# DLRM tower: GpSimd waits for the landing of one gather group before it issues the next

## The chip, the cores and the metric

The kernel runs on one core of one Trainium2 chip. The metric is device microseconds (us) of a whole execution. PE is TensorE, DVE is VectorE, ACT is ScalarE, POOL is GpSimd, SP is SyncE.

## The reference, cut to what matters

A batch of 2048 samples. Each has 26 ids, one into each embedding table (128 floats a row), and a dense vector of 128 floats. All in fp32:

```python
e = jnp.stack([tbl_f[ids[:, f]] for f in range(26)], axis=1)       # gather: 2048 x 26 x 128
combined = concatenate([dense[:, None, :], e], axis=1)             # 2048 x 27 x 128
z = einsum('bfd,bgd->bfg', combined, combined)[:, iu, ju]          # 351 pairs of each sample
h = relu(concatenate([z, dense], axis=1) @ W_top1 + b_top1)        # 479 -> 512
h = relu(h @ W_top2 + b_top2)                                      # 512 -> 256
y = h @ W_top3                                                     # 256 -> 1
```

## The kernel before

The batch is cut into 16 tiles of 128 samples. Two tiles (t = 0 and 1) make a turn s, and there are 8 turns. Turn 0 is written out; turns 1 to 7 run in a hardware loop on PE and ACT.

**Two kinds of features.** Ten tables of 1000 rows are "hot": they stay in SBUF, and PE fetches their rows by multiplying with one-hot matrices, for both tiles of the turn at once (`hot`, L449 to L463; 32 matmuls for each of 5 pairs of features, line L458). DVE makes the one-hot matrices (`compare`, L269 to L282, line L277). The other 16 tables are "cold": POOL gathers their rows from HBM by indirect DMA, one DMA of 128 rows for each tile and feature, into the one buffer `rows` (line L252, the loop L246 to L255). PE transposes these rows in `transposes` (L465 to L473, line L472), ACT copies what comes out to `feats` (L361 to L369).

**Groups.** `rows` holds 17 features of one tile: the dense vector (f = 0, loaded by SP, L193) and 16 cold ones. `GROUPS` (L40) cuts them in five: g0 has 3 gathers and the dense vector, g1, g2 and g3 have 4 gathers each, g4 has one. So a tile has 16 gathers and 5 groups, the whole kernel 256 gathers and 80 groups. Both tiles of a turn use the same `rows`: POOL may gather into group g of a tile when PE has transposed group g of the tile before (`wait_rows_free`, L154). Each group and tile of the turn has its own semaphore `gathered[t][g]`; each gather adds 16 to it when it has landed, and PE waits for it at L469.

**Order of the work.** It is written out by hand in `STEPS` (L56). In each turn PE does for tile 0: hot pair 0, rows g0, hot pair 1, rows g1 and so on to rows g4; then the first half of layer 1 (lines L496 to L498) of the turn before and the gram of tile 0. The gram is 512 small matmuls (L483). Then, for tile 1: rows g0, second half of layer 1 (of the turn before), rows g1, rows g2, layer 2 (L540), rows g3, rows g4, layer 3 (L548), and the gram of tile 1. ACT works through the same list with its copies, with the relu (L378) behind each layer. Behind each gram ACT and DVE copy the products out, and SP moves the pairs to `pairs` by nine DMAs (L176); SP also loads the ids of the next turn (L189). PE transposes groups g3 and g4 of tile 1 only after layer 2.

**What POOL does.** Only the gathers and the waits in front of them. All waits are conditions on semaphores that others raise; no other engine waits for POOL but by the landing of its gathers.

**The names below.** "Chain of gathers of turn s": POOL's gathers for tile 0 of turn s. It begins when PE has transposed group g0 of tile 1 of turn s - 1. The chains begin at 55.68, 118.09, 179.59, 238.81, 297.44, 355.94 and 414.16 us for turns 1 to 7.

Of the kernel before, what the change touches and what calls it, by code (L numbers as in the profile page):

```python
# [8 lines left out]
def dlrm_tower(nc, ids, dense, tables, ident, hot_ids, hot_tables, hot_rows, w1, b1, w2, b2, w3, out):  # L9
# [30 lines left out]
    GROUPS = [list(range(g, min(g + 4, NR))) for g in range(0, NR, 4)]  # L40
    NG = len(GROUPS)
# [19 lines left out]
    with ctx:  # L61
# [3 lines left out]
        def sem(name):  # L65
            return ctx.enter_context(nc.semaphore(name))
# [42 lines left out]
        gathered = [[sem(f"gathered{t}_{g}") for g in range(NG)] for t in range(2)]  # L109
# [40 lines left out]
        def wait_rows(eng, s, t, g):  # L150

            eng.wait_ge(rows_done, 2 * NG * s + NG * t + g + 1)

        def wait_rows_free(eng, s, t, g):  # L154

            if t == 1:
                wait_rows(eng, s, 0, g)
            elif s > 0:
                wait_rows(eng, s - 1, 1, g)
# [14 lines left out]
        def move_pairs(eng, t, pieces):  # L174
            for c, p0, n, j0, w in pieces:
                eng.dma_start(pairs[p0:p0 + n * w, c, t * P:(t + 1) * P],  # L176
                              gram[0:n, (j0 - 1) * P:(j0 - 1 + w) * P].rearrange(
                                  "i (j b) -> i j b", j=w)).then_inc(pairs_in[t], 16)
# [4 lines left out]
        @block.sync  # L183
        def _(sp):
            def load_ids(s, part):
                a, b = ((0, IDS_A), (IDS_A, NH))[part]
                if s > 0:
                    sp.wait_ge(compared, NH * (s - 1) + b)
                sp.dma_start(ids_b[:, a:b, :].rearrange("p f b -> p (f b)"),  # L189
                             hot_ids[s:s + 1, a * SB:b * SB].to_broadcast([P, (b - a) * SB])).then_inc(  # L190
                                 ids_in[part], 16)

            def load_dense(s, t):  # L193
                wait_rows_free(sp, s, t, 0)
                sp.dma_start(rows[:, 0, :], dense[2 * s + t, :, :]).then_inc(dense_in[t], 16)

            def wait_gram(s, t):
                if s == 0 and t == 0:
                    sp.wait_ge(zeroed, 1)
                elif s > 0:  # L200
                    sp.wait_ge(pairs_split, s)
                for h in range(2):
                    sp.wait_ge(gram_out[h], 4 * (2 * s + t + 1))

            def load_table(f):
                src = hot_tables[f].rearrange("(p c) d -> p c d", c=HC)
                for a, b in ((0, 112), (112, HP_ROWS)):
                    sp.dma_start(hot_raw[a:b, f, :, :], src[a:b, :, :]).then_inc(raw_in[f], 16)  # L208

            sp.dma_start(hot_rows_sb[0:HP_ROWS, :], hot_rows).then_inc(hot_rows_in, 16)  # L210
            sp.dma_start(idx[:, :, :], ids).then_inc(idx_in, 16)
            sp.dma_start(ident_sb[:, :], ident).then_inc(ident_in, 16)
            load_ids(0, 0)
            load_table(0)
            load_table(1)
            load_table(2)
            load_dense(0, 0)
            load_table(3)
            load_ids(0, 1)
            for f in range(4, NH):  # L220
                load_table(f)
            sp.dma_start(w1_raw, w1.rearrange("(c p) n -> p c n", p=P)).then_inc(raw_w1_in, 16)
            sp.dma_start(w2_sb[:, :, :], w2.rearrange("(c p) n -> p c n", p=P)).then_inc(weights_in, 16)
            sp.dma_start(w3_sb[:, :], w3).then_inc(weights_in, 16)
            sp.dma_start(b1_sb[:, :], b1).then_inc(weights_in, 16)
            sp.dma_start(b2_sb[:, :], b2).then_inc(weights_in, 16)

            for s in range(TURNS):
                load_dense(s, 1)
                if s + 1 < TURNS:  # L230
                    load_ids(s + 1, 0)
                wait_gram(s, 0)
                move_pairs(sp, 0, PIECES)
                if s + 1 < TURNS:
                    load_ids(s + 1, 1)
                    load_dense(s + 1, 0)
                wait_gram(s, 1)
                move_pairs(sp, 1, PIECES if s + 1 < TURNS else LAST_HERE)
            sp.wait_ge(y_out, TURNS)
            sp.dma_start(out, y).then_inc(stored, 16)  # L240
            sp.wait_ge(stored, 16)

        @block.gpsimd
        def _(pool):
            pool.wait_ge(idx_in, 16)
            for s in range(TURNS):  # L246
                for t in range(2):
                    for g, features in enumerate(GROUPS):
                        wait_rows_free(pool, s, t, g)
                        for f in features:  # L250
                            if f > 0:
                                pool.indirect_dma_start(  # L252
                                    out=rows[:, f, :], out_offset=None, in_=tables[f - 1],
                                    in_offset=bass.IndirectOffsetOnAxis(ap=idx[:, 2 * s + t, f - 1:f], axis=0),
                                ).then_inc(gathered[t][g], 16)  # L255
# [407 lines left out]
```

## Time and profile before

| | |
|---|---|
| median of 3 runs | 511.42 us (511.13 to 512.32) |
| the profiled execution, its own time | 512.17 us |
| its span, first to last instruction | 510.4 us |
| mean granted TensorE clock | 0.839 of full |
| PE busy | 360.0 us (71%), 6224 matmuls |
| DVE busy | 242.9 us (48%) |
| POOL busy | 254.2 us (50%), 256 of its 260 instructions gathers |
| ACT busy | 153.6 us (30%) |
| HBM read | 29.97 MB, 59 GB/s over the span |

Busy time is the time in which an engine has an instruction at work. A wait is put down to the instruction that released it; "remote" means that the profile found none that could have, "issue" that nothing it shows was waited for. The busy time of a gather on POOL is the making of its descriptors; the data move afterwards.

### The profile page before, as it was taken

Reading aid. Unit: us, or ns where it says so; the run is one execution under the profiler, and the core shown is the slowest. Engines: PE = TensorE matmul, PEld = TensorE weight load, DVE = VectorE, ACT = ScalarE, POOL = GpSimd, SP = SyncE. Lnnn points to the kernel's source line nnn. Section 1 sums busy time; section 2 is a strip of 40 time slices with the busy share of each in tenths; the row PEclk is TensorE's granted clock in tenths of the full one; section 3 lists DMA queues with packets and bytes.
Section 4 is the critical chain, followed back from the end, with each engine's and each line's share of the span. In section 5 each row is a group of like instructions: output and inputs, shape, how many; then the busy total and the mean of one; then the engine's idle time right before and its main releaser. Section 6 shows DMA issues by size and latency. Waiting matters only on the chain.

```text
span 510.4 us, 13987 instructions
## 1 busy us (share of the span) xinstructions
PE 360.0 (71%) x6224; PEld 332.2 (65%) x6224; DVE 242.9 (48%) x172; ACT 153.6 (30%) x269; POOL 254.2 (50%) x260
## 2 busy tenths in 40 slices
PE   7695516977279763989369782897459882798927
PEld 6583406966179762989259781896439881797826
DVE  4995703827048270745429370673509451380220
ACT  2462401234122331324132241233232341223512
POOL 5887560655506474265635755264734745165000
PEclk9988656999569995899759986898959986698978
DMA  7992230211202131121303112131312112111000
GB/s 198 251 278 54 55 90 7 79 43 51 78 17 80 36 87 46 34 65 39 94 26 77 46 45 79 29 74 31 102 31 66 47 41 84 26 54 41 16 15 1
DMA packets 23322, 33.32 MB, mean 65 GB/s; under 512 B 6565, under 2 KB 15397, under 8 KB 23303
## 3 DMA queue, kind: packets, MB, share of 16 engines
q0 software_dynamic: 8192, 16.79, 12.6%
q1 hardware_dynamic: 14926, 16.20, 11.8%
q8 instruction: 12, 0.20, 0.2%
q10 hardware_dynamic: 186, 0.09, 0.1%
q14 instruction: 6, 0.05, 0.0%
HBM read 29.97 MB, written 0.01 MB: 59 GB/s over the span
## 4 chain that ended last, share of the span: by engine, by line
PE 56%; issue 18%; another core or an unknown queue 14%; ACT 7%; DMA 3%; SPq 2%; DVE 1%; ACTq 0%; DVEq 0%
PE psum L458 31%; PE psum L483 11%; PE psum L472 3%; DMA lows<-table 3%; ACT feats L336 3%; PE psum L548 3%; PE psum L496 2%; PE psum L497 2%; PE psum L498 2%; ACT gram L336 2%; PE psum L540 1%; ACT h L378 1%; SPq L208 1%; ACT dense_hi L336 1%
## 5 line engine op out<-in xcount | busy, mean ns | idle before, releaser
L252 POOL DMA_INDIRECT rows<-table,idx x256 | 254.0, 992 | 215.0 <-PE psum L472 114.2
L277 DVE TENSOR_TENSOR onehot<-ids_b,psum 125x2048 fp32r<-125x2048 int16 x80 | 180.2, 2283 | 18.5 <-PE psum L458 12.3
L260 DVE COPY gram<-psum 26x416 f32<-26x416 f32 x64 | 37.4, 584 | 182.6 <-PE psum L483 181.1
L336 ACT ACTIVATE feats<-psum 128x512 f32<-128x512 f32 (+1 forms) x120 | 77.4, 689 | 148.1 <-PE psum L458 106.9
L458 PE MATMUL psum<-onehot,hot_hi 125*128 125x256 f32 x640 | 99.2, 299 | 11.1 <-issue 6.8
L483 PE MATMUL psum<-feats 128*26 128x26 f32 x4096 | 64.3, 211 | 59.6 <-issue 55.7
L483 PEld LDWEIGHTS psum<-feats 128*26 128x26 f32 x4096 | 55.9, 125 | 70.8 <-issue 64.8
L458 PE MATMUL psum<-onehot,hot_lo 125*128 125x256 f32 x640 | 95.6, 291 | 4.4 <-issue 4.3
L458 PEld LDWEIGHTS psum<-onehot,hot_hi 125*128 125x128 f32 x640 | 86.5, 200 | 14.2 <-issue 9.0
L458 PEld LDWEIGHTS psum<-onehot,hot_lo 125*128 125x128 f32 x640 | 86.7, 198 | 6.3 <-issue 5.6
L336 ACT ACTIVATE gram<-psum 26x416 f32<-26x416 f32 (+1 forms) x72 | 35.5, 494 | 73.1 <-PE psum L483 54.5
L548 PE MATMUL psum<-h,w_sb 128*1 128x256 f32 x32 | 13.2, 560 | 60.2 <-ACT h L378 60.2
L378 ACT ACTIVATE h<-psum,b_sb 128x256 f32<-128x256 f32 x44 | 18.4, 470 | 102.2 <-remote 78.4
L548 PEld LDWEIGHTS psum<-h,w_sb 128*1 128x1 f32 x32 | 2.5, 99 | 66.4 <-ACT h L378 62.2
L472 PE MATMUL psum<-ident_sb,rows 128*128 128x128 f32 x272 | 42.0, 282 | 0.0
L496 PE MATMUL psum<-pairs_hi,w_hi 126*128 126x256 f32 (+1 forms) x96 | 28.5, 297 | 9.0 <-DVE pairs_lo L286 9.0
L472 PEld LDWEIGHTS psum<-ident_sb,rows 128*128 128x128 f32 x272 | 32.9, 145 | 1.2
L540 PE MATMUL psum<-h,w_sb 128*128 128x256 f32 x128 | 29.0, 379 | 0.0
L286 DVE TENSOR_TENSOR pairs_lo<-pairs,pairs_hi 126x768 fp32r<-126x768 f32 x8 | 7.9, 987 | 43.3 <-ACT pairs_hi L336 34.3
L497 PE MATMUL psum<-pairs_lo,w_hi 126*128 126x256 f32 (+1 forms) x96 | 28.2, 294 | 0.0
L498 PE MATMUL psum<-pairs_hi,w_lo 126*128 126x256 f32 (+1 forms) x96 | 28.1, 293 | 0.0
L540 PEld LDWEIGHTS psum<-h,w_sb 128*128 128x128 f32 x128 | 23.7, 190 | 2.9
(26 smaller groups left out, 167.7 us busy)
## 6 DMA issues: line engine op xcount, KB each, us to landing
lows<-table SPq DMA_DIRECT2D x10, 448.0 KB
rows<-table,idx POOLq DMA_INDIRECT x256, 2.5
ids_b<-hot_ids SPq DMA_DIRECT2D x8, 384.0 KB
ids_b<-hot_ids SPq DMA_DIRECT2D x8, 256.0 KB
rows<-dense SPq DMA_DIRECT2D x16, 64.0 KB
lows<-w SPq DMA_DIRECT2D x1, 1024.0 KB
pairs<-gram SPq DMA_DIRECT2D x16, 39.0 KB
lows<-table SPq DMA_DIRECT2D x10, 52.0 KB
```

Source lines behind the costliest of these rows:

```text
L252: pool.indirect_dma_start(out=rows[:, f, :], out_offset=None, in_=tables[f - 1], in_offset=bass.IndirectOffsetOnAxis(ap=idx[:, 2 * s + t, ...
L260: return nc.vector.tensor_copy(o, x)
L277: nc.vector.tensor_tensor(onehot[f % SLOTS][0:HP_ROWS, :, :], ids_b[0:HP_ROWS, f:f + 1, :].to_broadcast([HP_ROWS, HC, SB]), psum[0:HP_ROWS ...
L336: return nc.scalar.activation(o, x, ACT.Copy)
L458: mm = nc.tensor.matmul(psum[:, bank, (f % 2) * SB:(f % 2 + 1) * SB], part[0:HP_ROWS, f, c, :], onehot[f % SLOTS][0:HP_ROWS, c, :], start= ...
L472: mm = nc.tensor.transpose(psum[:, bank, m * P:(m + 1) * P], rows[:, f, :], ident_sb[:, :])
L483: mm = nc.tensor.matmul(psum[32 * q:32 * q + NJ, GP[h], k * NJ:(k + 1) * NJ], feats[:, t, n, 0:NJ], feats[:, t, n, 1:NF], start=True, stop ...
L496: nc.tensor.matmul(o, w_hi, x_hi, start=(n == 0), stop=False)
L497: nc.tensor.matmul(o, w_hi, x_lo, start=False, stop=False)
L498: return nc.tensor.matmul(o, w_lo, x_hi, start=False, stop=(n == ZC))
L540: mm = nc.tensor.matmul(psum[:, HP[0], m * SB:(m + 1) * SB], w2_sb[:, c, m * P:(m + 1) * P], h1[:, c, :], start=(c == 0), stop=(c == C1 - 1))
L548: mm = nc.tensor.matmul(psum[0:1, HP[1], 0:SB], w3_sb[:, m:m + 1], h2[:, m, :], start=(m == 0), stop=(m == C2 - 1))
```

## The change

POOL gets one more wait at the head of each group. `wait_landed` waits until all gathers of the group in front of it (in POOL's order, across tiles and turns too) have added their 16 to their semaphore. The first group of all has none in front.

```diff
         @block.gpsimd
         def _(pool):
+            def wait_landed(s, t, g):
+
+                if g > 0:
+                    t0, g0, s0 = t, g - 1, s
+                else:
+                    t0, g0, s0 = 1 - t, NG - 1, s - (t == 0)
+                if s0 >= 0:
+                    pool.wait_ge(gathered[t0][g0], 16 * sum(f > 0 for f in GROUPS[g0]) * (s0 + 1))
+
             pool.wait_ge(idx_in, 16)
             for s in range(TURNS):
                 for t in range(2):
                     for g, features in enumerate(GROUPS):
                         wait_rows_free(pool, s, t, g)
+                        wait_landed(s, t, g)
                         for f in features:
                             if f > 0:
                                 pool.indirect_dma_start(
```

## Rows read from the trace of the kernel before

**Rows 1.** The page: shares of the chain that ended last.

```profile
PE 56%; issue 18%; another core or an unknown queue 14%; ACT 7%; DMA 3%; SPq 2%; DVE 1%; ACTq 0%; DVEq 0%
```

**Rows 2.** The page's costliest groups: busy us, mean ns of one | idle before, releaser.

```profile
L252 POOL DMA_INDIRECT rows<-table,idx x256 | 254.0, 992 | 215.0 <-PE psum L472 114.2
L483 PE MATMUL psum<-feats 128*26 128x26 f32 x4096 | 64.3, 211 | 59.6 <-issue 55.7
L378 ACT ACTIVATE h<-psum,b_sb 128x256 f32<-128x256 f32 x44 | 18.4, 470 | 102.2 <-remote 78.4
```

**Rows 3.** Waits: who waited for whom, us in total, times, longest.

```profile
POOL rows L252 <- PE psum L472: 114.2, 21, 14.4
POOL rows L252 <- remote: 30.1, 13, 3.0
```

**Rows 4.** Timeline of POOL in turn 4, to turn 5's next chain: start us, us, what [idle before].

```profile
297.44 0.94 POOL L252 DMA_INDIRECT rows<-table,idx  x1 [5.10 <-PE psum L472]
...
299.94 0.94 POOL L252 DMA_INDIRECT rows<-table,idx  x1 [0.30 <-issue]
301.19 0.94 POOL L252 DMA_INDIRECT rows<-table,idx  x1 [0.30 <-issue]
...
310.25 0.95 POOL L252 DMA_INDIRECT rows<-table,idx  x1 [0.30 <-issue]
314.18 0.94 POOL L252 DMA_INDIRECT rows<-table,idx  x1 [2.98 <-remote]
...
319.18 0.94 POOL L252 DMA_INDIRECT rows<-table,idx  x1 [0.30 <-issue]
328.73 0.94 POOL L252 DMA_INDIRECT rows<-table,idx  x1 [8.61 <-PE psum L472]
...
350.05 0.94 POOL L252 DMA_INDIRECT rows<-table,idx  x1 [0.30 <-issue]
355.94 0.94 POOL L252 DMA_INDIRECT rows<-table,idx  x1 [4.94 <-PE psum L472]
```

**Rows 5.** Line L252: gathers from issue (start on POOL) to landing.

```profile
DMA to landing us min/median/max: 2.5/2.5/4.4
```

**Rows 6.** Timeline of PE in the same stretch.

```profile
304.22 0.71 PE L472 MATMUL psum<-ident_sb,rows 128*128 128x128 f32 x5
314.77 1.44 PE L548 MATMUL psum<-h,w_sb 128*1 128x256 f32 x3 [9.84 <-ACT h L378]
...
316.43 0.71 PE L483 MATMUL psum<-feats 128*26 128x26 f32 x35
317.57 0.33 PE L483 MATMUL psum<-feats 128*26 128x26 f32 x6 [0.43 <-issue]
...
321.16 2.59 PE L483 MATMUL psum<-feats 128*26 128x26 f32 x200 [1.11 <-issue]
...
327.85 0.60 PE L472 MATMUL psum<-ident_sb,rows 128*128 128x128 f32 x4
```

**Rows 7.** Timeline of ACT in the same stretch: the relu behind layer 2.

```profile
313.88 0.84 ACT L378 ACTIVATE h<-psum,b_sb 128x256 f32<-128x256 f32 x2 [9.68 <-remote]
```

**Rows 8.** Timeline of PE in the last turn, with POOL at rest.

```profile
480.41 0.71 PE L472 MATMUL psum<-ident_sb,rows 128*128 128x128 f32 x5
481.50 1.02 PE L548 MATMUL psum<-h,w_sb 128*1 128x256 f32 x4 [0.38 <-ACT h L378]
482.43 2.56 PE L483 MATMUL psum<-feats 128*26 128x26 f32 x256
```

**Rows 9.** Timeline of POOL: chains of turn 1 and turn 7, first and last gathers.

```profile
6.21 0.95 POOL L252 DMA_INDIRECT rows<-table,idx  x1 [0.30 <-issue]
...
55.68 0.94 POOL L252 DMA_INDIRECT rows<-table,idx  x1 [3.69 <-PE psum L472]
...
74.41 0.94 POOL L252 DMA_INDIRECT rows<-table,idx  x1 [0.30 <-issue]
...
414.16 0.94 POOL L252 DMA_INDIRECT rows<-table,idx  x1 [4.86 <-PE psum L472]
...
468.43 0.94 POOL L252 DMA_INDIRECT rows<-table,idx  x1 [0.30 <-issue]
```

**Rows 10.** Timeline of PE in turn 0: first transposes, and the gram of tile 1.

```profile
15.71 0.60 PE L472 MATMUL psum<-ident_sb,rows 128*128 128x128 f32 x4
...
58.98 0.55 PE L483 MATMUL psum<-feats 128*26 128x26 f32 x42 [1.12 <-ACT feats L336]
...
78.71 2.34 PE L483 MATMUL psum<-feats 128*26 128x26 f32 x179 [0.50 <-issue]
```

**Rows 11.** Stretch 5 to 38 us: busy PE, PEld, DVE, ACT, POOL; clock, DMA share, GB/s.

```profile
5.00:38.00 33.00, 27.16 (x180) 24.98 (x178) 30.25 (x19) 15.62 (x18) 26.60 (x22) 0.95 1.04 264
```

## The prediction

> **What bounds the kernel now.** I read the chain of waits first. Only 56% of it is PE at work; 18% is "issue" and 14% an unknown queue [rows 1]. So the span holds a good part in which PE has nothing to do that the program names. The costliest groups say where: the gram matmuls sat 55.7 us in "issue", and ACT's relu waited 78.4 us for something "remote" [rows 2]. POOL is busy only half the span, and it waited 114.2 us for PE's transposes and 30.1 us for "remote" [rows 3]. Now the timelines of turn 4. PE's records put layer 2 and the transposes of g3 and g4 of tile 1 before 304.93 (304.22 + 0.71) [rows 6], but ACT's relu, which needs only layer 2, starts at 313.88 [rows 7], and POOL, which needs only the g3 transposes, at 314.18 [rows 4]. Two engines agree: what PE finished by 304.9 was not seen until about 313.9, 9 us later. Then the gram of tile 1, 256 matmuls, runs in scraps (35, 6, ... matmuls with gaps) and gets free only at 321.16 [rows 6].
>
> The last turn runs the same loop code on PE, but there POOL is at rest: its last gather is issued at 468.43 [rows 9]. There layer 3 follows the transposes of 480.41 at 481.50, with no hold, and the gram takes 2.56 us in one piece [rows 8]. DVE's comparisons and SP's id loads for a next turn are absent there too, so this contrast alone does not say which of them is to blame. The second sign is better: the scraps follow POOL. In turn 4 the hold ends 3.6 us after the last gather of an unbroken run (310.25 to 313.88), the gram is free 2.0 us after the next run's last one (319.18 to 321.16) [rows 4, 6, 7]. In turn 0 the gram of tile 1 starts freely at 58.98, is cut off at 59.53, and gets free at 78.71, 4.3 us after the last of 16 dense gathers (74.41) [rows 9, 10]: some 20 us for 2.6 us of work. And it begins late: the cut comes 3.85 us after that run's first gather (55.68 to 59.53), in turn 4 3.0 us after (314.18 to 317.14) [rows 4, 6, 9, 10]. So I read: an unbroken run of gathers stalls PE, from 3.0 to 3.85 us after its first issue until 2.0 to 4.3 us after its last. How, no row says.
>
> **The change, part by part.** Nothing is removed. POOL gets 79 waits. Inside a run, gathers start 1.25 us apart (299.94 to 301.19, over a group's edge) [rows 4]. With the wait, the next group's first starts after the landing of the last one before: 2.5 us by the median [rows 5], and a wake-up, for which I take POOL's 0.28 us behind PE's transposes (327.85 + 0.60 to 328.73) [rows 4, 6]. That is 2.75, so 1.5 us more for each group edge, 79 x 1.5 = 119 us in all. Bounds for one landing: 2.5 and 4.4 us [rows 5]. Behind POOL's wait only gathers are queued; who waits for them is PE's transposes alone.
>
> The Trainium skill (DMA: Bandwidth & Descriptors, Anatomy of one DMA, SWDGE path) gives a GpSimd DMA about 2.0 us fixed plus bytes over 436 GB/s, an estimate of 2.15 us for a gather of 64 KB. The trace has 2.5, a little more, and that is used; by the page's figure POOL's floor below would be 80 x 0.35 = 28 us lower.
>
> POOL's own floor: a tile has 16 gathers in 5 groups, 11 steps of 1.25 and 5 of 2.75 = 27.5 us; a turn has 55.0. Some gathers take longer than 0.944 us (the total of 254.0 is 12.3 us above 256 x 0.944 [rows 2, 4]), most in turn 0; I add 0.5 a turn: 55.5. Now a turn takes 355.94 - 297.44 = 58.5 us [rows 4]. So POOL, which had slack, becomes the bound, yet below today's turn, if PE keeps up. Would it? After the change a group's last issue is followed by 2.75 us of nothing and then at least 3.0 us before a cut: a free stretch from 2.0 to 4.3 until 5.75 to 6.6 us behind each last issue, 1.5 to 4.6 us of each 6.5. That releases the held layer 2 (due at 304.9) at the edge it falls on instead of after 9 us, and gives the gram its 2.6 us in one or two pieces. PE's turn without the hold (9.0) and with the gram of tile 1 at 2.6 instead of the 7.3 from 316.43 to 323.75 [rows 6] is 58.5 - 9.0 - 4.7 = 44.8 us, 11 under POOL's 55.5. I take it that PE keeps up.
>
> Start: POOL begins at 3.6 and has two tiles of 27.5: 58.6. Between 5 and 38 us the DMA engines are full (share 1.04, 264 GB/s) [rows 11], and landings are late: g0's last was issued at 6.21 and had landed by 15.71 at the latest [rows 9, 10], so 2.5 to 9.5 us. Four edges lie there. I take 5.0 each, nearer the middle since at most four gathers then stand in the queue: +10; stretched gathers +4. Chain of turn 1 at 72.6 (bounds 58.6 to 91) against 55.68: +17.
>
> Turns 1 to 6: 6 x 55.5 = 333.0 against 414.16 - 55.68 = 358.5 [rows 9]: -25.5. Turn 7's chain to its last landing: 55.2 against 468.43 + 2.5 - 414.16 = 56.8: -1.6. Then the tail. Before, PE transposes the last groups at 481.12, 10.2 us after the last landing, because it was late itself [rows 8, 9]; after, it is waiting for them and does so 0.9 us after the landing: -9.3. From there to the end the same 29.3 us. Sum: +17 - 25.5 - 1.6 - 9.3 = -19.4. Against the profiled execution's 512.17 (span 510.4 and 1.8 around it) 492.8; this execution stands 0.75 above the median of the runs, so **492 us**.
>
> **The rivals.**
> (a) Landings come later than the median. From this case's sum: 0.1 us on each landing costs 7 us over 7 turns of 10 edges, so from 2.5 + 19.4/70 = 2.8 us on the kernel is slower than before. The 4.4 of [rows 5] is for it, that the median equals the minimum is against it. At 3.0 us it gives 492 + 35 = 527.
> (b) The pauses don't free PE, since it takes a rest longer than they leave (the 4.3 us of turn 0 is for it, the 2.0 and 3.6 of turn 4 and the late cut against). Then each edge is added to the path: the end of the hold moves by two edges (3.0), the gram's release by three (4.5), and the gram of tile 0, which waits out the run that ends at 350.05, by 8.6 (those 4.5 and four edges more, 6.0, less 1.9 that lie in POOL's waits) [rows 4, 6]. A turn takes 67, and 512 + 6.5 x 8.6 + 10 for the start = 578. It decides from the point where a run's stall outlasts the 5.75 us.
> (c) Same: PE is held by something else (DVE's comparisons, the id loads), and 1.5 us at an edge fits in POOL's 144 us of waits [rows 3]; but not all of the edges lie beside them. 508 to 516.
> (d) Landings get shorter when fewer gathers are under way, or the start costs nothing: 475 to 480.
>
> The Trainium skill (same page, Rules for kernel authors) says to issue a DMA early and to wait for it late, so that the fixed cost overlaps. The change waits at once, 79 times. Rivals (a) and (b) are what that rule would give here. The trace agrees with it in that the extra POOL time is real, and disagrees in that the dense issue has a price of its own on PE.
>
> **How the numbers follow.** The forecast case 0.55, with a range of its own of 480 to 508 (landings 0.1 us either way, the start 10 us either way); (a) 0.18, (b) 0.13, (c) 0.09, (d) 0.05. Runs of this kernel can tell 0.2% (1 us) from no change. Faster: 0.55 + 0.05 and 0.02 of (c) = 0.62; the same 0.05; slower 0.18 + 0.13 + 0.02 of (c) = 0.33. The range runs from 480 to 538: it takes in most of (a) and all of (c), and leaves out (b) and (d).
>
> **What would show it.** In POOL's timeline: starts 2.7 to 2.8 us apart at every group edge, waits that end on a landing and hardly any on PE's transposes. A chain every 55.5 us. ACT's relu behind layer 2 within 3 us of PE's record of it, the 78.4 us of "remote" gone to under 30, the gram's 55.7 us of "issue" under 25. PE idle before the transposes instead, and a lower granted clock. In turn 0 the chain of turn 1 begins near 72.6. It is wrong if POOL still waits for PE at the g3 group (rival b), if edges measure 3 us or more (rival a), or if the relu is held as before with POOL pausing (rival c).

## The result, and the profile after

The changed kernel takes 549.41 us (median of 4 runs, 549.14 to 554.35), the kernel before 511.87 us beside it (4 runs, 511.13 to 512.34): a ratio of 1.0761, 95% interval 1.0708 to 1.0815. It is slower by 7.6%. The forecast was 492 us and faster; the time is also above the range.

The profiled execution of the changed kernel took 554.35 us, with a span of 552.5. The chain of waits, where [rows 1] had PE at 56%:

```profile
DMA 36%; POOL 26%; issue 19%; PE 17%; SPq 1%; DVE 1%; ACT 0%; POOLq 0%; DVEq 0%; ACTq 0%
```

The end is now set by POOL's gathers and their landings. The costliest groups (against [rows 2]; busy us, mean ns of one | idle before, releaser):

```profile
L262 POOL DMA_INDIRECT rows<-table,idx x256 | 247.8, 968 | 272.9 <-DMA rows<-table,idx 166.3
L493 PE MATMUL psum<-feats 128*26 128x26 f32 x4096 | 82.7, 211 | 79.8 <-issue 76.5
L388 ACT ACTIVATE h<-psum,b_sb 128x256 f32<-128x256 f32 x44 | 18.4, 470 | 44.2 <-PE psum L508 21.1
```

The waits, us in total, times, longest (against [rows 3]):

```profile
POOL rows L262 <- DMA rows<-table,idx: 166.3, 61, 7.3
...
PE psum L482 <- DMA rows<-table,idx: 57.2, 20, 5.9
...
POOL rows L262 <- PE psum L482: 34.2, 13, 4.7
```

POOL waits 166.3 us for landings and hardly for PE: of the 13 waits put down to PE, 11 are edges of 3.2 to 3.4 us like those put down to a landing (at 395.90 below, for one). PE waits 57.2 us for gathered rows, which it did not before. POOL's timeline in turn 4 (start us, us, what [idle before]), against [rows 4]:

```profile
333.70 0.94 POOL L262 DMA_INDIRECT rows<-table,idx  x1 [2.26 <-PE psum L482]
...
336.20 0.94 POOL L262 DMA_INDIRECT rows<-table,idx  x1 [0.30 <-issue]
339.43 0.94 POOL L262 DMA_INDIRECT rows<-table,idx  x1 [2.29 <-DMA rows<-table,idx]
...
350.19 0.96 POOL L262 DMA_INDIRECT rows<-table,idx  x1 [0.30 <-issue]
354.37 0.94 POOL L262 DMA_INDIRECT rows<-table,idx  x1 [3.23 <-DMA rows<-table,idx]
...
395.90 0.94 POOL L262 DMA_INDIRECT rows<-table,idx  x1 [2.35 <-PE psum L482]
```

Over a group's edge the starts are 3.23 us apart (336.20 to 339.43), at the worst edge of the tile 4.18 (350.19 to 354.37). The turn takes 395.90 - 333.70 = 62.2 us (the mean of turns 1 to 6 is 63.3), where it took 58.5 before and 55.5 in the forecast. PE at the same time (against [rows 6]):

```profile
333.98 0.73 PE L493 MATMUL psum<-feats 128*26 128x26 f32 x43
335.02 0.24 PE L493 MATMUL psum<-feats 128*26 128x26 f32 x3 [0.32 <-issue]
335.74 0.26 PE L493 MATMUL psum<-feats 128*26 128x26 f32 x5 [0.48 <-issue]
...
337.91 1.86 PE L493 MATMUL psum<-feats 128*26 128x26 f32 x142 [1.16 <-issue]
340.00 0.30 PE L493 MATMUL psum<-feats 128*26 128x26 f32 x5 [0.23 <-issue]
```

The gram of tile 1 is still in scraps, some five matmuls in each 0.73 us while a group's gathers are issued. In POOL's pause after 336.20 it runs freely from 337.91 to 339.77, and is cut 0.6 us after the next group's first gather (339.43 to 340.00). Its first 43 ran freely beside gathers too. (A gram is 256 matmuls, 4096 for 16 tiles; the 512 given in the description of the kernel are those of a turn.)

The start of the run, the chain of turn 7 and the last gather (against [rows 9]):

```profile
6.20 0.94 POOL L262 DMA_INDIRECT rows<-table,idx  x1 [0.30 <-issue]
14.40 0.94 POOL L262 DMA_INDIRECT rows<-table,idx  x1 [7.25 <-DMA rows<-table,idx]
...
79.35 0.94 POOL L262 DMA_INDIRECT rows<-table,idx  x1 [2.26 <-PE psum L482]
...
459.20 0.94 POOL L262 DMA_INDIRECT rows<-table,idx  x1 [2.26 <-PE psum L482]
...
520.15 0.94 POOL L262 DMA_INDIRECT rows<-table,idx  x1 [4.66 <-PE psum L482]
```

The prediction's terms against the two profiled executions:

| term | forecast | measured |
|---|---|---|
| chain of turn 1 begins later | +17 | 79.35 - 55.68 = +23.7 |
| turns 1 to 6 | -25.5 | 379.85 - 358.48 = +21.4 |
| chain of turn 7 to its last landing (last issue + 2.5) | -1.6 | 63.45 - 56.8 = +6.7 |
| tail | -9.3 | 29.9 - 39.5 = -9.6 |
| sum | -19.4 | +42.2 (spans: 552.5 - 510.4 = 42.1) |

The profiled execution stands 4.9 us above the median, so the medians are 37.5 apart.

**Two times of the kernel before.** One thing must be known to read the experiments. In most of the later comparisons the kernel before took 382 to 387 us, not 512. In the first measurement, in that of `each` (513.89) and in that of `small_compare`, `nogather_b`, `latechain_b` and `two_ahead_b` (510.83) it took 508 to 515. Within a comparison it never changed (9 and 13 runs in two of them), so ratios hold inside one. The number of the chip doesn't tell the two apart (number 6 gave 384.10 once and 510.83 later). I call them the 512 place and the 385 place. Of the 127 us between them PE's busy time makes 23 (360.0 us in the 512 place, at a granted clock of 0.839; 336.8 in `extra` below, the stand-in for the kernel before in the 385 place, at 0.964); the rest is time in which PE sits idle. The gathers land in 2.5 us by the median in both. What makes the two places is open.

### The profile page after: what moved, and what is told of

Read it like the earlier page. It is cut to its first block, busy times and chain, and to the rows that moved or that the text cites. A ratio compares the mean times of both kernels' runs of the same rounds, so it can differ in the third digit from the quotient of the medians.

```text
span 552.5 us, 14062 instructions
## 1 busy us (share of the span) xinstructions
PE 393.6 (71%) x6224; PEld 355.3 (64%) x6224; DVE 242.9 (44%) x172; ACT 154.8 (28%) x269; POOL 248.0 (45%) x260
## 4 chain that ended last, share of the span: by engine, by line
DMA 36%; POOL 26%; issue 19%; PE 17%; SPq 1%; DVE 1%; ACT 0%; POOLq 0%; DVEq 0%; ACTq 0%
DMA rows<-table,idx 35%; POOL rows L262 26%; PE psum L468 9%; PE psum L493 3%; PE psum L482 2%; PE psum L558 1%; PE psum L550 1%; SPq L176 1%; DMA pairs<-gram 1%; PE psum L506 0%; DVE gram L270 0%; DMA idx<-ids 0%; PE psum L507 0%; PE psum L508 0%; DVE pairs_lo L296 0%
## 5 line engine op out<-in xcount | busy, mean ns | idle before, releaser
L262 POOL DMA_INDIRECT rows<-table,idx x256 | 247.8, 968 | 272.9 <-DMA rows<-table,idx 166.3
L493 PE MATMUL psum<-feats 128*26 128x26 f32 x4096 | 82.7, 211 | 79.8 <-issue 76.5
L493 PEld LDWEIGHTS psum<-feats 128*26 128x26 f32 x4096 | 64.3, 124 | 99.4 <-issue 93.8
L468 PE MATMUL psum<-onehot,hot_hi 125*128 125x256 f32 x640 | 104.7, 311 | 5.4 <-DVE onehot L287 2.5
L468 PEld LDWEIGHTS psum<-onehot,hot_hi 125*128 125x128 f32 x640 | 92.4, 213 | 8.3 <-DVE onehot L287 4.5
L482 PE MATMUL psum<-ident_sb,rows 128*128 128x128 f32 x272 | 50.8, 312 | 57.9 <-DMA rows<-table,idx 57.2
L482 PEld LDWEIGHTS psum<-ident_sb,rows 128*128 128x128 f32 x272 | 35.6, 157 | 64.7 <-issue 30.2
L388 ACT ACTIVATE h<-psum,b_sb 128x256 f32<-128x256 f32 x44 | 18.4, 470 | 44.2 <-PE psum L508 21.1
L506 PEld LDWEIGHTS psum<-pairs_hi,w_hi 126*128 126x128 f32 (+1 forms) x96 | 21.8, 227 | 9.1 <-DVE pairs_lo L296 9.1
L550 PEld LDWEIGHTS psum<-h,w_sb 128*128 128x128 f32 x128 | 23.7, 190 | 2.9
L507 PEld LDWEIGHTS psum<-pairs_lo,w_hi 126*128 126x128 f32 (+1 forms) x96 | 21.7, 226 | 0.1
L508 PEld LDWEIGHTS psum<-pairs_hi,w_lo 126*128 126x128 f32 (+1 forms) x96 | 21.5, 224 | 0.0
```

Source lines behind the costliest of these rows:

```text
L262: pool.indirect_dma_start(out=rows[:, f, :], out_offset=None, in_=tables[f - 1], in_offset=bass.IndirectOffsetOnAxis(ap=idx[:, 2 * s + t, ...
L388: nc.scalar.activation(dst[:, c, :], psum[:, bank, n * SB:(n + 1) * SB], ACT.Relu, bias=bias[:, c:c + 1]).then_inc(relu_out, 1)
L468: mm = nc.tensor.matmul(psum[:, bank, (f % 2) * SB:(f % 2 + 1) * SB], part[0:HP_ROWS, f, c, :], onehot[f % SLOTS][0:HP_ROWS, c, :], start= ...
L482: mm = nc.tensor.transpose(psum[:, bank, m * P:(m + 1) * P], rows[:, f, :], ident_sb[:, :])
L493: mm = nc.tensor.matmul(psum[32 * q:32 * q + NJ, GP[h], k * NJ:(k + 1) * NJ], feats[:, t, n, 0:NJ], feats[:, t, n, 1:NF], start=True, stop ...
L506: nc.tensor.matmul(o, w_hi, x_hi, start=(n == 0), stop=False)
```

## Experiments

The theories after the result. Theory 1: the term for a group's edge was too small, since the new wait is an instruction of its own, where the one that it was priced from rides on a gather; POOL's turn sets the time. Theory A: a dense run of gathers stalls PE. Its rivals: DVE's comparisons, the id loads or memory traffic do. The expectations number their theories anew for each run; where that matters, the text says which is meant. Of the code of each edit only the lines that matter are shown.

**again.** The changed kernel, nothing edited, with others beside it.

> The changed kernel once more, beside the kernel before, since on the chip of the runs 'swap' to 'latechain' the kernel before took 385 us and not 512. Theory A (the change makes POOL the bound, on any chip): 545 to 555 us here too, with group edges of 3.2 us, whatever the kernel before takes. Theory B (the changed kernel is slow only where PE is stalled): it moves with the kernel before, to about 1.07 of it, 413 us where that takes 385.

549.18 us (547.08 to 554.2), before 384.10: ratio 1.4279 (1.4217 to 1.4341). The changed kernel takes 549 us in both places, and the kernel before doesn't. In the 385 place its grams hardly wait (6.2 us of "issue" for 76.5), and its time is the same: what PE gains there doesn't shorten POOL's chain. The chain of waits at one edge (start us, us, what):

```profile
383.46 2.53 DMA rows<-table,idx
385.99 0.02 issue
386.02 0.02 POOLq L252
386.03 0.72 issue
386.75 0.94 POOL rows L262
```

The landing is seen at 385.99; the wait (its line is L252) is an instruction of its own and ends at once; the next gather starts 0.76 us after the landing.

**swap and swap_b.** The same wait, one line higher.

```diff
-                        wait_rows_free(pool, s, t, g)
                         wait_landed(s, t, g)
+                        wait_rows_free(pool, s, t, g)
```

> The changed kernel with its two waits at the head of a group in the other order: landing first, transposes second. Nothing else differs. Theory 1: a group edge of 3.25 us (last issue to next group's first) is 2.5 us of landing and 0.74 us because the landing wait is an instruction of its own in front of the gather (record of it 0.74 us before the gather's start), while the wait on the transposes rides on the gather itself and costs only 0.28 us. In the other order the landing wait rides on the gather: edges of 2.8 us, 79 x 0.45 = 36 us less, about 514 us. Theory 2: a landing always costs POOL 0.75 us until the next start, in whatever form it is waited for: edges stay at 3.25, 549 us.

> The change with its two waits in the other order, once more. Theory A: POOL's turn sets the time of this kernel, so it takes 505 to 511 wherever it runs; where the kernel before takes 512 that is about the same or 1% faster. Rival: where PE is stalled beside dense gathers, this kernel loses to it as well, and takes 530 or more there. Where before takes 385 it gives 508 as in the first run of it, and tells nothing new.

508.02 us (506.08 to 509.87), before 385.39: ratio 1.3194 (1.3136 to 1.3252). The second time 506.64 (506.23 to 509.08), before 384.37: 1.3203 (1.3133 to 1.3273); it met the 385 place again, so its question stays open. Where two waits are written ahead of a gather, the first rides on the gather and the second becomes an instruction of its own: in the changed kernel the landing wait, here the wait for PE. The edge of `swap`:

```profile
250.78 0.94 POOL L262 DMA_INDIRECT rows<-table,idx  x1 [0.30 <-issue]
253.54 0.94 POOL L262 DMA_INDIRECT rows<-table,idx  x1 [1.81 <-DMA rows<-table,idx]
```

2.76 us, the landing of 2.5 and 0.26. Nothing else was edited, and the kernel is 41 us faster than `again`, both in the 385 place (36 were expected). Theory 1 holds. Both kernels have 75 waits that are instructions of their own; in `swap` they hardly ever block. The changed kernel has one such edge itself, in tile 0 of turn 0, where there is no wait for PE yet and the landing wait rides:

```profile
42.23 0.94 POOL L262 DMA_INDIRECT rows<-table,idx  x1 [0.30 <-issue]
44.96 0.94 POOL L262 DMA_INDIRECT rows<-table,idx  x1 [1.78 <-DMA rows<-table,idx]
```

2.73 us there, 3.2 and more at all edges behind it. Why a wait of its own takes half a microsecond more, the trace doesn't show.

**extra.** The kernel before with a wait at each group's head that is always met.

```diff
                         wait_rows_free(pool, s, t, g)
+                        pool.wait_ge(idx_in, 16)
```

> The kernel before, with one more wait at the head of each group, on the ids of the gathers, which landed at the start: the instruction without any waiting. Theory 1 (a separate wait instruction costs the gather behind it 0.4 to 0.5 us): the start-to-start distance over a group edge grows from 1.25 to about 1.7 us, and the time by 0 to 10 us, since POOL had waits of 144 us: 512 to 522 us. Theory 2 (the price belongs to the landing): edges stay at 1.25 to 1.3 us and the time at 511.9.

384.55 us, before 385.39: 0.9996 (0.9971 to 1.0022). Group edges stay 1.25 us. So the first expectation for this run, that the mere instruction widens an edge to 1.7 us, missed. A wait of its own costs nothing if it doesn't block; the 0.76 us fall due when it does. This run is also the trace for the kernel before in the 385 place:

```profile
PE 336.8 (88%) x6224; PEld 311.5 (82%) x6224; DVE 241.2 (63%) x172; ACT 152.7 (40%) x269; POOL 253.0 (66%) x260
...
PE 77%; POOL 9%; issue 7%; DMA 2%; ACT 2%; SPq 1%; DVE 1%; POOLq 0%; DVEq 0%; ACTq 0%
...
L484 PE MATMUL psum<-feats 128*26 128x26 f32 x4096 | 55.6, 195 | 12.9 <-issue 4.6 <-ACT feats L337 3.3
```

PE is busy 88% of the span and makes 77% of the chain.

**less_pe.** The changed kernel without half of the one-hot matmuls.

```diff
-                    for part in (hot_hi, hot_lo):
+                    for part in (hot_hi,):
```

> The changed kernel with half of the one-hot matmuls (those with hot_lo, 640 of 6224, 92 to 96 us of PE's busy time) left out in all turns. Theory A (POOL's chain of issues and landings sets the time): 540 to 550 us, within 2% of the changed kernel. Rival (PE is a bound too, its stalls or its clock): 10 us or more of the 92 come back for each 10% that PE holds, under 535 us.

552.62 us, before 384.73: 1.437 (1.4231 to 1.4509). PE's busy time falls from the 374.3 of `again` to 321.2 us and the kernel gains nothing. PE is no bound of the changed kernel in the 385 place. In the 512 place this edit wasn't run; there the chain of waits and the equal time of 549 us say the same.

**small_ids.** The changed kernel with the id loads of turns 1 to 7 cut to one partition.

```diff
-                sp.dma_start(ids_b[:, a:b, :].rearrange("p f b -> p (f b)"),
+                rows_to = P if s == 0 else 1
+                sp.dma_start(ids_b[0:rows_to, a:b, :].rearrange("p f b -> p (f b)"),
```

> The changed kernel, with the id loads of turns 1 to 7 (384 and 256 KB, spread over 128 partitions) cut to one partition; DVE compares stale ids there. Theory A: the landings of 3.0 to 4.1 us instead of 2.5, one or two in each tile, are late because of these loads: they go, 14 times 0.9 = 13 us less, 536 us. Rival: they are late beside the moves of the pairs (nine DMAs of SP, 7.2 us, by 512 bytes): unchanged, 549 us.

547.83 us, before 384.84: 1.4235 (1.3978 to 1.4492). The late landings (3.0 to some 4 us, one or two a tile) stay, so the id loads don't make them. They lie in SP's stretch of pair moves, as in the changed kernel in turn 4, from 348.24 on, with the edge of 354.37 in it:

```profile
348.24 7.26 SPq L176 DMA_DIRECT2D pairs<-gram  x9
```

That these moves delay the landings wasn't tried.

**two_edges.** The kernel before with the landing wait of the change at two edges a turn, from turn 1 on.

```diff
+                        if t == 0 and g in (1, 2) and s > 0:
+                            wait_landed(s, t, g)
```

> The kernel before with landing waits at only two edges of a turn: in front of g1 and g2 of tile 0, where the trace of 512 us showed PE held for 9 us. Each costs POOL 2.0 us. Where the kernel before takes 385 us, PE is not held and POOL's waits for PE are under 4 us a turn: 4 us a turn on POOL show up at most in part, 385 to 410. Where it takes 512: theory A, pauses free PE: the held relu comes up to 5 us earlier, 480 to 505; theory B, they don't: 3 to 4 us later per turn, 530 to 540.

402.38 us, before 384.06: 1.0482 (1.039 to 1.0575). 18.3 us for 14 edges, 1.3 each: even 14 of the 79 waits cost. The question for the 512 place, whether two pauses free PE, wasn't met.

**two_ahead and two_ahead_b.** The wait for the group two in front, ahead of `wait_rows_free`.

```diff
+                n = 2 * NG * s + NG * t + g - 2
+                s0, t0, g0 = n // (2 * NG), n // NG % 2, n % NG
```

> The changed kernel waiting for the group two in front (so two groups may be under way), landing wait first. A group of four takes 5.0 us to issue, longer than the 2.5 us of a landing; only behind g4, which has one gather, a wait of 1.25 us is left: POOL turns of 40 + 2.5 us, no bound. Theory A (the price is POOL's alone): within 1% of the kernel before on the same chip. Rival (any landing wait costs the path): 3% or more above it.

> The wait for the group two in front. Where before takes 512: if the stall comes from gathers being dense, not from how many are under way, 500 to 525, for the gathers stay 1.25 us apart. Rival (outstanding gathers stall PE): below 450. Where before takes 385: 394.

385 place: 394.33 us, before 384.10: 1.0265 (1.0236 to 1.0293). 512 place: 526.50, before 510.83: 1.032 (1.0234 to 1.0406). The first lies between the theories' 1% and 3%, the second just above the 500 to 525 of its first theory and far from the rival's 450. Most edges are back at 1.25 us; behind the lone gather of g4, where only one gather lies between the wait and what it waits for, they are 1.5 to 2.5 in the 385 place. In the 512 place the grams still sit 64.6 us in "issue". So limiting POOL to two groups frees nothing. It doesn't test how many single gathers may be under way: with 1.25 us from issue to issue and 2.5 us to a landing there are about two, here as in the kernel before.

**nogather and nogather_b.** The kernel before with the gathers of turn 0 only; PE waits for those alone.

```diff
-            for s in range(TURNS):
+            for s in range(1):
```

> The kernel before without the gathers of turns 1 to 7; PE's transposes wait only for those of turn 0, so turns 1 to 7 work on stale rows. All of DVE, ACT, SP and PE is the same. Theory 1 (gathers under way stall PE): no 9 us between PE's record of layer 2 and ACT's relu, grams of 2.6 us in one piece, turns of about 45 us instead of 58.5: some 420 us. Rival (the comparisons on DVE or the id loads hold PE): the 9 us and the scraps stay, turns of 55 us or more, above 485 us.

> The kernel before without the gathers of turns 1 to 7 (they use turn 0's rows). Theory A: about 370 us whatever before takes on this chip, grams in one piece. Rival (comparisons or id loads stall PE): about 500 where before takes 512. Where before takes 385, 370 as in the run of this kernel before, which tells nothing more.

385 place: 370.01 us, before 385.39: 0.9596 (0.9564 to 0.9628). 512 place: 371.68, before 510.83: 0.7285 (0.7206 to 0.7365). The 420 us first expected were reckoned for the 512 place before the other was known; the second expectation, 370, came true. Without gathers the two places are the same within 0.5%. The comparisons and the id loads are all there, and the grams don't stall. So the gathers, directly or by what hangs on them, make all of the difference between 385 and 512.

**small_compare.** The kernel before with the comparisons of turns 1 to 7 cut to an eighth.

```diff
+                n = HC if first else 1
-                    onehot[f % SLOTS][0:HP_ROWS, :, :],
+                    onehot[f % SLOTS][0:HP_ROWS, 0:n, :],
```

> The kernel before with DVE's comparisons of turns 1 to 7 cut to an eighth of their columns (so the one-hot matrices are not made anew there). The question is what holds PE's small matmuls where the kernel before takes 512 us. Theory A: dense gathers do; then this stays near 500 or more where before takes 512, with PE's grams still in scraps. Rival: the comparisons do, then the time falls toward 390 and the grams run in one piece. Where before takes 385, PE is the bound and this gives 380 to 385, which tells nothing of the question.

509.51 us, before 510.83, both in the 512 place: 0.996 (0.9922 to 0.9998). DVE is busy 114.8 instead of 242.9 us, and the grams stall as before, where without gathers they don't. `small_compare`, then `nogather_b`:

```profile
L484 PE MATMUL psum<-feats 128*26 128x26 f32 x4096 | 66.2, 211 | 61.9 <-issue 58.2 <-ACT feats L337 3.7
```

```profile
L483 PE MATMUL psum<-feats 128*26 128x26 f32 x4096 | 42.0, 194 | 15.5 <-issue 11.2 <-ACT feats L336 4.4
```

**latechain and latechain_b.** The kernel before, the chain of each turn held until the gram of tile 1 is done.

```diff
+                        if s > 0 and t == 0 and g == 0:
+                            pool.wait_ge(gram_done[1], 2 * s)
```

> The kernel before, but POOL begins a turn's chain of gathers only when PE has finished the gram of tile 1 of the turn before, instead of when it has transposed g0 of tile 1. No landing waits. Theory 1 (gathers under way stall PE): layer 2 and the gram of tile 1 now run with POOL at rest, so the 9 us hold and 4.7 us of scraps go; the gram of tile 0 is stalled longer, since POOL's 40 us of issue start about 10 us later in the turn. About 57 us a turn against 58.5: 500 us, 485 to 510. Rival (something else holds PE): the hold stays and the gathers come later, 520 us or more.

> The kernel before, with the chain of gathers of each turn held until the gram of tile 1 is done. Theory A where before takes 512: 480 to 510, since the second gram runs free of gathers and the relu behind layer 2 comes in time. Rival (gathers do not stall PE): 540 or more, since the chain is later by 8 to 10 us a turn and nothing is given back. Where before takes 385: about 418.

385 place: 418.37 us, before 385.39: 1.088 (1.081 to 1.095). 512 place: 533.33, before 510.83: 1.0454 (1.0337 to 1.0571). For the 512 place both expectations for dense gathers missed (485 to 510 and 480 to 510): 533 lies in the first rival's range (520 or more) and under the second's (540 or more), but the trace shows theory A's stall in another place. POOL's gathers run unbroken from 384.16, 16 for tile 0 and three for tile 1, the last issued at 406.62; PE in the 512 place:

```profile
392.64 1.00 PE L460 MATMUL psum<-onehot,hot_lo 125*128 125x256 f32 x7
395.63 0.28 PE L460 MATMUL psum<-onehot,hot_lo 125*128 125x256 f32 x1 [2.00 <-issue]
397.05 0.37 PE L474 MATMUL psum<-ident_sb,rows 128*128 128x128 f32 x1 [1.14 <-issue]
399.13 0.37 PE L474 MATMUL psum<-ident_sb,rows 128*128 128x128 f32 x1 [1.71 <-issue]
...
409.63 0.37 PE L460 MATMUL psum<-onehot,hot_hi 125*128 125x256 f32 x1 [1.72 <-issue]
...
443.36 2.46 PE L485 MATMUL psum<-feats 128*26 128x26 f32 x256
```

The gram of tile 1 runs in one piece. But the one-hot matmuls and transposes, under which the chain now lies, drop to one in about 2 us from 393.6, 9.5 us into the run, until 411.7, 5.1 us after its last issue. In the 385 place PE does the same work beside a chain with no such gaps, at full pace:

```profile
301.48 1.12 PE L460 MATMUL psum<-onehot,hot_hi 125*128 125x256 f32 x8
302.44 1.12 PE L460 MATMUL psum<-onehot,hot_lo 125*128 125x256 f32 x8
305.07 0.65 PE L474 MATMUL psum<-ident_sb,rows 128*128 128x128 f32 x4 [1.51 <-DMA rows<-table,idx]
```

The stall isn't avoided by moving the chain; it falls on what lies beside it.

**traffic.** The kernel before with five copies of 1 MB from HBM to HBM in each turn, on ACT's queue.

```diff
+                            act.wait_ge(spilled, 16 * (5 * s + k))
+                        act.dma_start(spill, w1).then_inc(spilled, 16)
```

> The kernel before with five copies of 1 MB from HBM to HBM in each turn, issued by ACT (behind hot pairs 1 and 3, around both grams), 40 MB more in all. It asks what made the kernel before take 512 us in the first measurement and 385 in all later ones. Theory A (PE was held because the DMA engines or HBM were loaded beside the dense gathers): the grams run in scraps of some 5 matmuls each 0.7 us and ends of PE's work are seen late, as in the trace of 512 us; 440 us or more. Theory B (it is no load that the kernel can make itself): the grams stay in one piece (issue waits of L483 under 30 us), the time grows by late landings only, 385 to 420.

403.71 and 411.9 us, before 384.03. The two runs lie 2% apart; by the lower, which is the one of the trace, the load costs some 20 us, without an interval. Gathers land in 4.1 us by the median instead of 2.5, but the grams don't fall into scraps (10.4 us of "issue"). So this traffic, and landings as late as these, don't turn the 385 place into the other. Traffic of other cores wasn't tried.

**each.** The changed kernel with the landing wait behind every gather but the last.

```diff
+                                if n > 0:
+                                    pool.wait_ge(gathered[t][g], 16 * (sum(x > 0 for x in features) * s + n))
```

> The changed kernel with a landing wait behind every gather, 255 instead of 79. Theory A (POOL's chain is the time: a step with a wait 2.5 + 0.75 us for a group's edge, 2.5 + 0.3 us inside a group, where the landing wait rides on the gather): 176 steps grow from 1.25 to 2.8 us, 273 us more: 820 us. Rival (landings get shorter when a single gather is under way, down to its 2.0 us): 176 x 1.0 = 180 us more, 730 us.

825.81 us, before 513.89: 1.6056 (1.5888 to 1.6225), as the first of its two theories expected (820). The waits within a group ride on the gathers:

```profile
300.02 0.95 POOL L263 DMA_INDIRECT rows<-table,idx  x1 [1.78 <-DMA rows<-table,idx]
302.76 0.95 POOL L263 DMA_INDIRECT rows<-table,idx  x1 [1.79 <-DMA rows<-table,idx]
305.44 0.95 POOL L263 DMA_INDIRECT rows<-table,idx  x1 [1.74 <-DMA rows<-table,idx]
308.63 0.95 POOL L263 DMA_INDIRECT rows<-table,idx  x1 [2.24 <-DMA rows<-table,idx]
```

2.7 us a step inside, 3.2 at the group's edge, in one kernel side by side. And in the 512 place the grams now wait only 13.0 us in "issue". A gram beside the gather issued at 314.57:

```profile
313.32 1.60 PE L494 MATMUL psum<-feats 128*26 128x26 f32 x108
315.15 0.33 PE L494 MATMUL psum<-feats 128*26 128x26 f32 x6 [0.23 <-issue]
315.90 1.55 PE L494 MATMUL psum<-feats 128*26 128x26 f32 x136 [0.43 <-issue]
```

One gather still cuts it, 0.6 us after its issue and for 0.7 us of gaps around one scrap, and then it is free until the next. Gathers 1.25 us apart leave it no free stretch, gathers 2.7 us apart do. The waits change two things at once, though: the distance, and that one gather is under way at a time instead of about two. Which of them counts wasn't tried.

## Why the prediction was wrong

**The step that failed is "That is 2.75, so 1.5 us more for each group edge".** The shape (landing plus wake-up) was right. The size of the wake-up was read from POOL's wait for PE's transposes, 0.28 us, which rides on the gather [rows 4, 6]. In the traces one wait rides on a gather, and the new one became an instruction of its own; with it, the next gather starts 0.76 us after the landing. The edge is 3.26 us, not 2.75. `swap` changes just this and is 41.2 us faster (549.18 to 508.02), `extra` shows that it is not the instruction, but its blocking, and `each` has both prices in one trace. Why blocking there costs 0.5 us more stays open. This is 41 of the 57 us between forecast and result.

**The other 16 us, which `swap` still lacks to 492,** are landings and the start. Turn 4 after: 22 steps of 1.25 are 27.5 us, eight edges near 3.26 are 26.0, and two of 4.18 and 4.12 are 8.3; one stretched gather adds 0.4: 62.2. Of the 6.7 us over the forecast, ten edges give 5.1 by the wake-up, two of them 1.8 more by landings of 3.4, and the stretched gather stays 0.1 under what was allowed for. I had used the median of 2.5 with its maximum of 4.4 beside it [rows 5], as rival (a), which was given 0.18: "from 2.8 us on slower". Rival (a) had the right point of decision: edges above its limit of 3 us make the kernel slower. But its cause, late landings, is the smaller part; the longer wake-up stood in no rival. That 549 lies between the 527 of (a) and the 578 of (b) is to the credit of neither. At the start the first landing took 7.9 us (6.20 to 14.40, less 0.26), the two behind it 7.6 and 5.6, against 5.0 taken.

**That POOL becomes the bound was right** (chain of waits, `less_pe`), and so was the tail (-9.6 for -9.3). But then a turn can't be shorter than POOL's own, and every tenth at an edge counts 79 times. Rival (a) deserved more than its 0.18.

**PE's relief was half right and worth nothing.** The relu behind layer 2 lost its hold (102.2 us idle to 44.2 [rows 2]). The grams did not: "under 25" was forecast for their "issue", and it went from 55.7 to 76.5. The error is the late onset, "3.0 to 3.85 us after its first issue". In these traces some 43 matmuls run freely when a gram begins beside gathers already under way (43 from 333.98, the gather having been issued at 333.70; 42 in turn 0 [rows 10]), so the first 43 said nothing of the onset. For small matmuls the cut comes 0.6 us after a group's first gather (339.43 to 340.00), so the pause of each edge frees them for less than 2 us (337.91 to 339.77), in a gram that needs 2.6 and gets some five in each 0.73 us otherwise. One-hot matmuls and transposes were stalled only well into a long run (from 393.6 in `latechain_b`); the prediction made no such difference.

**That gathers stall PE was right in the 512 place** (`nogather_b`, `small_compare`, `each`); rival (c) falls with `nogather_b`, where comparisons and id loads are all there, and for the comparisons with `small_compare` too. It isn't a property of the kernel alone: in the 385 place the same gathers don't do it, and the change costs 43% there for 7.6%. The time that stalled PE loses, 127 us in all, exists in one place only, and there too only gathers as far apart as in `each` were seen to free the grams for the most part, which POOL can't afford: 256 of them at 2.75 us are 704 us.

**Open:** what sets the two places (the load that other cores put on the memory, and the recording of the profile itself, were not tried); whether `swap` would beat the kernel before in the 512 place (508.0 and 506.6 measured in the other, against 511.9 here; if POOL is its bound there too, as it is for the changed kernel, it would be level or 1% faster); and what ties PE's issue to POOL's gathers: their issue on POOL or their data, their distance or their overlap, and whether PE lacks instructions or something else. No version tried that does the whole work beats the kernel before where both were measured. The nearest that waits for landings is `two_ahead`, 2.7 and 3.2% slower.

The Trainium skill (DMA: Bandwidth & Descriptors, Rules for kernel authors) says to issue early and wait late; the runs agree, with 1.5 us for each edge where the wait rides and 2.0 where it stands alone.

## What to carry to other kernels

A wait for a landing on the engine that issues the transfers turns its latency into that engine's issue time. Count the edges, price each as landing plus wake-up less the step that it replaces, with the tail of the landings and not their median, and compare the sum with the turn of today's bound before anything else. Look at which instruction carries the wait: of two written ahead of one instruction, the first rode here, so the one that will block belongs first. Reckon a wait's wake-up from a wait of the same form. And if a kernel's profile shows "issue" and "remote" on its bound, run it again at another time before designing against it.

## What the runs showed of the hardware

- The same wait on POOL: 0.26 us from landing to the next gather where it rides on the gather, 0.76 where it is an instruction of its own and blocks, nothing where it is met.
- The kernel before takes 382 to 387 or 508 to 515 us, constant within a comparison. The difference needs the gathers (370.0 and 371.7 without them), and it doesn't need the comparisons (`small_compare`).
- In the 512 place a single gather cuts a gram 0.6 us after its issue, for 0.7 us (`each`); beside gathers 1.25 us apart PE issues some five small matmuls in each 0.73 us, and from 9.5 us into an unbroken run one transpose or one-hot matmul in some 2 us (`latechain_b`).
- A gather of 64 KB landed in 2.5 us by the median in both places, in 3.0 to some 4 us at one or two edges a tile of the changed kernel, in 4.1 by the median beside copies of 1 MB (`traffic`), and in 5.6 to 7.9 before 38 us, where the DMA engines were busy for 0.96 of the time (1.04 before [rows 11]).
